# Graph network kernel, first layer: overflow tiles compared out of column numbers in the third section, instead of loaded in the last

## The chip, the core and the metric

One Trainium2 chip, one of its cores. The core has a matrix engine (PE, TensorE), a vector engine (DVE, VectorE), an activation engine (ACT, ScalarE), a general engine (POOL, GpSimd) and a queue engine (SP, SyncE) that here only issues transfers. They run their own instruction streams and meet at semaphores. The metric is device microseconds of one execution, the median of several runs.

## What is computed

Four graph layers over 12,500 nodes with 64 features and 212,500 directed edges, each behind a layer norm and added to x. The second of them (`_L1_gnn_ref`) is the one that matters here: four rounds of a graph convolution over the same graph.

```python
def _L1_gnn_ref(x, edge_index, Ws, bs, ln_w, ln_b):
    deg = jnp.zeros((n,), x.dtype).at[dst].add(1.0) + 1.0
    dinv = jax.lax.rsqrt(deg)
    enorm = (dinv[src] * dinv[dst])[:, None]
    self_norm = (dinv * dinv)[:, None]
    h = x
    for l in range(Ws.shape[0]):
        hw = h @ Ws[l]
        agg = jnp.zeros_like(hw).at[dst].add(enorm * hw[src])
        agg = agg + self_norm * hw + bs[l]
        mean = jnp.mean(agg); var = jnp.mean(jnp.square(agg - mean))
        h = jax.nn.relu(ln_w[l] * (agg - mean) * jax.lax.rsqrt(var + EPS) + ln_b[l])
    return h
```

The last graph layer (`_L2_gnn_ref`) sums messages over the same edges and ends in a small network per node; the kernel does it at the end with the same matrix of edge counts.

## The kernel before, in words

**The matrix.** The kernel sums messages with matrix products. It writes the edges into a dense matrix of counts `adj` in device memory, one byte for each pair of nodes: 98 tiles of 128 source rows by 12,544 columns. A count of 256 or more doesn't fit a byte. Each time a pair's running count reaches a multiple of 256, the kernel writes a one into one of seven more row tiles instead, the overflow tiles (rows 98 to 104 of tiles, `NJ` to `AB`, `NV` = 7). Row p of overflow tile k has at most one such event: `row_f[p, k]` holds the source node, or -1, and `vcol[p, k]` the destination node, which is the column of the one. The stationary operand that goes with overflow tile k is the features of those source nodes times 256; POOL gathers them from `node_table` (`virtual_rows`, line 951) and ACT and DVE split them into three bf16 terms (`virtual_terms`).

**The scatter.** POOL writes the matrix, edges sorted by source row: `adj_out` (line 934) issues 1,664 indirect DMAs of 128 one-byte cells, in NB = 52 blocks of 32. After each block, as it lands, `cells_landed` raises `cells_in`. The order on POOL is: blocks 0 to 14; gathers for another part; blocks 15 to 47; `virtual_rows(0, VT)`; blocks 48 to 51; the last `cells_landed`.

**The first of the four rounds** starts before the scatter is done. Its source rows are cut into nine sections (`CUTS` = 0, 30, 46, 60, 72, 80, 86, 91, 96, 98), and a section's loads on SP wait until the blocks that can touch its rows have landed (`chk`). Each section runs over seven groups of 1,792 destination columns; one section of one group is a unit, and has its own PSUM area of two that alternate. A tile is 128 rows by 1,792 columns, 224 KB of bytes. The path of tile n is: SP loads it to `RAW[n % 5]` (line 770) once the buffer is converted; DVE (n % 5 = 1 or 3) or ACT (0, 2, 4) converts it to bf16 in `RING[n % 5]` once PE has freed that; PE multiplies it in 12 products (`products`, line 1322): three terms, two column parts, two halves. A unit's sum is added to `FM` by `add_part` on DVE; in the last section `scaled` adds it, multiplies by `DINVB` and takes statistics (lines 2596 to 2605). `DINVB` comes by two transfers of SP per group (`group_end`, line 742), which wait until `scaled` has finished the group two before; the loads of the next unit stand behind them in SP's order. PE, too, starts a unit only when the group two before is through `scaled`.

DVE's conversion while POOL scatters is written as a multiply-add with a PSUM operand (line 2558), and as a plain copy (line 2556) from tile `LAST_FROM` = 672 on, which is the first of the last section. The last section has tiles 96 and 97 and the seven overflow tiles, nine per unit, 63 in all. All nine sections together are 735 tiles.

**Behind it** come statistics, three more rounds (lines 1342 and 2669) which load all 105 row tiles per group, and the last graph layer, in which the overflow tiles are already made by a comparison: line 2886 compares column numbers `iota_f` with `srj` (there the source node less 128 times the block number, since that layer sums the other way), a table of 7 by 14 columns that lines 2794 to 2797 make with 98 small instructions just before that layer's tiles.

Of the kernel before, what the change touches and what calls it, by code (L numbers as in the profile page):

```python
# [37 lines left out]
P = 128  # L38
GT = 7
# [28 lines left out]
def gnn_kernel(nc, n_nodes, n_edges, a, out):  # L68
# [22 lines left out]
    NCK = len(CUTS) - 1  # L91
    assert TILES % P == 0 and TILES % CB == 0 and NB % 4 == 0 and CUTS[1] > 0 and CB * P == 1 << 12
# [18 lines left out]
    with ctx:  # L111
# [146 lines left out]
        PART = [list(range(CUTS[c], CUTS[c + 1])) + (list(range(NJ, AB)) if c == NCK - 1 else []) for c in range(NCK)]  # L258
        UNIT = [(c, g) for c in range(NCK) for g in range(NJ // (2 * GT))]
        LAST_OF = [sum(len(PART[c]) for c, _ in UNIT[:u + 1]) - 1 for u in range(len(UNIT))]  # L260
        assert LAST_OF[-1] + 1 == NJ // (2 * GT) * AB
        LAST_FROM = LAST_OF[NJ // (2 * GT) * (NCK - 1) - 1] + 1
        VIRT_AT = LAST_OF[NJ // (2 * GT) * (NCK - 1) - 1] // NR
# [242 lines left out]
        def _(sp):  # L506
# [251 lines left out]
            for c in range(NCK):  # L758
# [4 lines left out]
                for g in range(NG2):  # L763
                    for K in PART[c]:
                        i, r = n % NR, n // NR
                        if i in BY_ACT:
                            sp.wait_ge(sem("conv_a"), r * NA + i // 2 + 1)
                        else:
                            sp.wait_ge(sem("conv_d"), r * ND + i // 2 + 1)
                        sp.dma_start(RAW[i], adj[K * P:(K + 1) * P, g * (2 * QW):(g + 1) * (2 * QW)]).then_inc(sem(f"ring_in{i}"), 16)  # L770
                        n += 1
# [63 lines left out]
        def _(pool):  # L835
# [117 lines left out]
            adj_out(NB // 4 + 2, NB - 4)  # L953
            virtual_rows(0, VT)
            adj_out(NB - 4, NB)
# [29 lines left out]
        def _(pe):  # L985
# [399 lines left out]
            def by_parts():  # L1385

                n = 0
                for u, (c, g) in enumerate(UNIT):
# [6 lines left out]
                    for K in PART[c]:  # L1395
# [8 lines left out]
                        products(stat, RING[i], base, x, K == CUTS[c], K == PART[c][-1]).then_inc(sem("ring_free"), 1)  # L1404
# [586 lines left out]
        def _(dve):  # L1991
# [469 lines left out]
            dve.sem_inc(sem("dve_at"), 1)  # L2461

# [87 lines left out]
            def to_bf16_first(r):  # L2550

                for i in BY_DVE:
                    dve.wait_ge(sem(f"ring_in{i}"), r * 16 + 16)
# [90 lines left out]

            split_terms(0)
            NOTHING = PS[:, 4 * 512:4 * 512 + 1]
            then(dve.memset(NOTHING, 0.0))
            AFTER = {(LAST_OF[u] + NR) // NR: u for u in range(len(UNIT) - 1)}
            assert len(AFTER) == len(UNIT) - 1
            for r in range(NG2 * NK):  # L2650
# [3 lines left out]
                if r in AFTER:  # L2654
                    if UNIT[AFTER[r]][0] < NCK - 1:
                        add_part(AFTER[r])
                    else:
                        scaled(AFTER[r])
# [135 lines left out]
            for k in range(NV):  # L2794
                for j in range(2 * GT):
                    t = dve.tensor_scalar(srj[:, k * 2 * GT + j:k * 2 * GT + j + 1], row_f[:, k:k + 1], float(-j * P), None, ALU.add)
            then(t)
# [153 lines left out]
```

## Time and profile before

| | |
|---|---|
| median of 3 runs | 9879.17 us (9872.16 to 9879.80) |
| the profiled execution, its own time | 9849.77 us |
| its span in the profile | 9847.9 us |
| first round, first product to last | 6040 to 6993 us of the span |
| its last section, first load to last statistics | 6908 to 6997 us |
| PE busy in the span | 7048.5 us (72%) |
| DVE busy | 7017.6 us (71%) |
| ACT busy | 4868.2 us (49%) |
| POOL busy | 5374.9 us (55%) |

The profile's times count from the start of the span. A busy share over the whole span says little here, since the kernel has stages with different limits. One reads first the chain that ended last, then, stage by stage, which engine had no gap and what the others waited for.

### The profile page before, as it was taken

What the parts mean: (1) busy time and instruction counts of PE and PEld (TensorE: products, weight loads), DVE (VectorE), ACT (ScalarE), POOL (GpSimd) and SP (SyncE); (2) the same over time, 40 slices, a digit from 0 to 9 for tenths busy, and PEclk for the clock granted to TensorE, in tenths of its full rate; (3) what the DMA queues carried; (4) which work ended last, traced back from release to release, by engine and by line L of the source; (5) the groups of instructions that cost most, each with busy time, mean ns of one, the idle gap of its engine ahead of it and who ended that gap; (6) DMA issues with size and microseconds to landing.
All of it is one profiled execution on the core that took longest, in us unless ns stands there. A gap on an engine that the chain in (4) does not pass through costs nothing.

```text
span 9847.9 us, 151767 instructions
## 1 busy us (share of the span) xinstructions
PE 7048.5 (72%) x44134; PEld 5763.7 (59%) x44134; DVE 7017.6 (71%) x18590; ACT 4868.2 (49%) x7967; POOL 5374.9 (55%) x5426
## 2 busy tenths in 40 slices
PE   4444444424888878872656567996899999997998
PEld 3333333313666667661445455664699898896887
DVE  7888888833666666662558777775688787787777
ACT  1111111112555555551442336885688787785787
POOL 5777777777777777777777777776000000000220
PEclk5555555555777776775776788998999999998999
DMA  5556544444333333339995896775788888886999
GB/s 192 195 194 196 175 143 143 144 134 66 93 92 93 92 93 93 94 92 93 266 229 123 188 216 175 204 204 123 221 281 281 248 280 252 275 281 177 210 218 198
DMA packets 2775520, 1739.57 MB, mean 177 GB/s; under 512 B 1805046, under 2 KB 2613980, under 8 KB 2774660
## 3 DMA queue, kind: packets, MB, share of 16 engines
q1 hardware_dynamic: 2435460, 1298.36, 52.3%
q10 hardware_dynamic: 165920, 277.72, 8.1%
q0 software_dynamic: 173408, 154.46, 6.8%
q8 instruction: 370, 6.06, 0.3%
q14 instruction: 362, 2.97, 0.1%
HBM read 1065.70 MB, written 506.69 MB: 160 GB/s over the span
## 4 chain that ended last, share of the span: by engine, by line
POOL 44%; PE 19%; issue 18%; DMA 9%; DVE 5%; ACT 3%; SPq 1%; POOLq 0%; DVEq 0%; ACTq 0%
POOL adj L934 16%; POOL records L908 13%; PE PS L1342 13%; POOL G L854 12%; DMA raw_f<-adj 3%; PE PS L1532 3%; DMA pair_raw<-adj 2%; DVE OH L2136 1%; ACT ring_f L1848 1%; DMA G<-node_table,IDX 1%; POOL fill_rows L870 1%; POOL T L885 1%; ACT ring_f L1971 1%; PE PS L1322 1%; POOL AG L885 1%
## 5 line engine op out<-in xcount | busy, mean ns | idle before, releaser
L854 POOL DMA_INDIRECT G<-node_table,IDX x1664 | 1626.1, 977 | 561.8 <-issue 551.3
L934 POOL DMA_INDIRECT adj<-OH,EA x1664 | 1652.5, 993 | 507.3 <-issue 507.3
L908 POOL DMA_INDIRECT records<-RT,IDX x1664 | 1614.0, 970 | 516.8 <-issue 499.6
L1342 PE MATMUL PS<-ring_f,terms_r 128*128 128x448 f32 x8232 | 1702.6, 368 | 17.3 <-DVE ring_f L2669 8.2
L2669 DVE CAST ring_f<-raw_f 128x1792 fp32r<-128x1792 uint8 x1323 | 1408.0, 1091 | 377.7 <-DMA raw_f<-adj 198.6
L1848 ACT CAST ring_f<-raw_f 128x1792 fp32r<-128x1792 uint8 x882 | 1465.5, 1691 | 380.0 <-DMA raw_f<-adj 249.5
L1342 PEld LDWEIGHTS PS<-ring_f,terms_r 128*128 128x128 f32 x8232 | 1537.3, 188 | 172.0 <-ACT ring_f L1848 19.3
L1187 PE MATMUL PS<-R 98*128 98x128 f32 x3328 | 995.1, 392 | 0.0
L2143 DVE TENSOR_TENSOR_SCAN S<-M,S,PS 128x512 f32<-128x512 bf16 x621 | 791.2, 1274 | 249.0 <-ACT PS L1737 224.2
L1102 PE MATMUL PS<-OH 128*98 128x128 bf16 x3328 | 453.3, 316 | 624.0 <-DVE OH L2136 624.0
L951 POOL DMA_INDIRECT HC<-node_table,srow x21 | 31.2, 1486 | 1510.4 <-issue 1510.4
L1102 PEld LDWEIGHTS PS<-OH 128*98 128x98 bf16 x3328 | 365.7, 198 | 781.8 <-DVE OH L2136 781.8
L2136 DVE TENSOR_SCALAR OH<-iota_b,AG 128x128 bf16<-128x128 bf16 (+1 forms) x4480 | 821.5, 283 | 0.0
L1638 ACT ACTIVATE PS<-PS,poolb 128x512 f32<-128x512 f32 x208 | 137.7, 662 | 1311.1 <-PE PS L992 1068.4
L2558 DVE SCALAR_TENSOR_TENSOR AG<-AG,PS 128x1792 bf16<-128x1792 uint8 x269 | 543.1, 2022 | 275.6 <-PE PS L1322 142.5
L2273 DVE TENSOR_TENSOR L<-PS,below 128x512 bf16<-128x512 f32 x416 | 285.7, 687 | 625.4 <-PE PS L1171 619.0
L968 POOL DMA_INDIRECT ends_b<-runs_e,endrow_src x98 | 144.4, 1474 | 1050.6 <-PE PS L1354 548.7
L1187 PEld LDWEIGHTS PS<-R 98*128 98x128 f32 x3328 | 715.3, 265 | 0.0
L1185 PE MATMUL PS<-OH 128*98 128x128 bf16 x1664 | 474.4, 285 | 316.6 <-ACT R L1672 314.9
L992 PE MATMUL PS<-ident,RT 128*128 128x128 f32 x832 | 232.0, 434 | 597.3 <-DVE RT L2160 592.7
L1532 PE MATMUL PS<-ring_f,terms_r 128*128 128x448 f32 x2744 | 608.9, 376 | 66.6 <-DVE ring_f L2883 31.5
L1971 ACT CAST ring_f<-pair_raw 128x1792 fp32r<-128x1792 uint8 x343 | 571.5, 1692 | 167.0 <-PE PS L1532 111.4
(416 smaller groups left out, 14498.8 us busy)
## 6 DMA issues: line engine op xcount, KB each, us to landing
raw_f<-adj SPq DMA_DIRECT2D x2205, 224.0 KB, 3.7
adj<-Z ACTq DMA_DIRECT2D x105, 1568.0 KB
AG<-adj SPq DMA_DIRECT2D x735, 224.0 KB
G<-records SPq DMA_DIRECT2D x624, 128.0 KB
M<-same_dst SPq DMA_DIRECT2D x416, 128.0 KB
fill_rows<-Z ACTq DMA_DIRECT2D x104, 512.0 KB, 2.8
runs_l<-R SPq DMA_DIRECT2D x208, 256.0 KB
G<-fill_rows SPq DMA_DIRECT2D x208, 256.0 KB
```

The source lines that it names most:

```text
L854: pool.indirect_dma_start(G[:, i, q * D:(q + 1) * D], None, table, bass.IndirectOffsetOnAxis(ap=IDX[:, i, q:q + 1], axis=0)).then_inc(sem( ...
L908: pool.indirect_dma_start(rec, bass.IndirectOffsetOnAxis(ap=IDX[:, i, q:q + 1], axis=0), RT[:, i, q, :], None).then_inc(sem(f"scattered{i} ...
L934: pool.indirect_dma_start(adj_cells, bass.IndirectOffsetOnAxis(ap=CELL[:, at:at + 1], axis=0), VAL[:, at:at + 1], None).then_inc(sem(f"cel ...
L1102: t = pe.matmul(hist_of(b, k % 2 if b == 0 else 0), OH[:, s, 2 * b, k, 0:NJ], OH[:, s, 2 * b + 1, k, :], start=False, stop=False, skip_gro ...
L1187: t = pe.matmul(bank(6 + x)[:, k * P:(k + 1) * P], OHTs[0:NJ, x, k * P:(k + 1) * P], Cs[0:NJ, k, :], start=False, stop=True, skip_group_ch ...
L1342: m = pe.matmul(half_of(x, h)[:, c, :], stat, RINGF[q % NR][:, h * QW + c * HW:h * QW + (c + 1) * HW], start=K == 0, stop=False, skip_grou ...
L1532: m = pe.matmul(half_of(0, h)[:, c, :], stat, RINGF[n % NE][:, h * QW + c * HW:h * QW + (c + 1) * HW], start=p == 0, stop=p == AB - 1, ski ...
L1848: act.copy(RINGF[q % NR][:, :], RAWF[q % NW][:, :]).then_inc(sem("conv_a"), 1)
L1971: act.copy(RINGF[n % NE][:, :], raw[:, 0:2 * QW, K % 2]).then_inc(sem("conv_a"), 1)
L2136: t = dve.tensor_scalar(OH[:, s, d, k, 0:w], iota_b[:, 0:w], key(d, q + k), None, ALU.is_equal)
L2143: return dve.tensor_tensor_scan(S[:, i % 2, :], mask, data, init, op0, op1)
L2669: dve.tensor_copy(RINGF[q % NR][:, :], RAWF[q % NW][:, :]).then_inc(sem("conv_d"), 1)
```

## The change

The overflow tiles of the first round are no longer loaded. DVE makes each by one comparison (`scalar_tensor_tensor`: column number `iota_f` plus the group's first column, is-equal `srj`), straight to the ring in bf16. They move from the last section to the third (index `EV_C` = 2), and lie there on ring buffers 1 and 3 alone. A unit of the third section has 21 tiles instead of 14, one of the last 2 instead of 9. SP raises the ring's semaphore for such a tile without a transfer.

So that the operands are there in time: `virtual_rows` moves on POOL from block 48 to block 36 (`EV_AT`), and `virtual_terms` from conversion round 134 to round 64 (`VIRT_AT`). Four small DVE instructions behind `srow_ready` work out `srj` early, from `vcol` (-1 where there is no event). The 98 small instructions before the last graph layer become one. `LAST_FROM` becomes 721. For the last section DVE's finishing of ended units (`close`) is done ahead of the next conversion when the unit's last tile lies five tiles back.

```diff
     NCK = len(CUTS) - 1
+    EV_C = 2
+    EV_AT = NB * 9 // 13
     assert TILES % P == 0 and TILES % CB == 0 and NB % 4 == 0 and CUTS[1] > 0 and CB * P == 1 << 12
...
-        PART = [list(range(CUTS[c], CUTS[c + 1])) + (list(range(NJ, AB)) if c == NCK - 1 else []) for c in range(NCK)]
         UNIT = [(c, g) for c in range(NCK) for g in range(NJ // (2 * GT))]
-        LAST_OF = [sum(len(PART[c]) for c, _ in UNIT[:u + 1]) - 1 for u in range(len(UNIT))]
+
+        def rows_of_units():
+            units, n = [], 0
+            for c, _ in UNIT:
+                nodes, events, rows = list(range(CUTS[c], CUTS[c + 1])), list(range(NJ, AB)) if c == EV_C else [], []
+                while nodes or events:
+                    rows.append((events if rows and events and n % NR in BY_DVE else nodes).pop(0))
+                    n += 1
+                units.append(rows)
+            return units
+
+        PART = rows_of_units()
+        LAST_OF = [sum(len(rows) for rows in PART[:u + 1]) - 1 for u in range(len(UNIT))]
+        EVENT = {sum(len(rows) for rows in PART[:u]) + x: (UNIT[u][1], K - NJ)
+                 for u in range(len(UNIT)) for x, K in enumerate(PART[u]) if K >= NJ}
+        assert len(EVENT) == NV * (NJ // (2 * GT)) and all(n % NR in BY_DVE for n in EVENT)
         assert LAST_OF[-1] + 1 == NJ // (2 * GT) * AB
         LAST_FROM = LAST_OF[NJ // (2 * GT) * (NCK - 1) - 1] + 1
-        VIRT_AT = LAST_OF[NJ // (2 * GT) * (NCK - 1) - 1] // NR
+        VIRT_AT = LAST_OF[NJ // (2 * GT) * EV_C - 1] // NR
...
             spread = [NJ * (k + 1) // NV if g else NJ - NR * (NV - 1 - k) for k in range(NV)]
...
                 for g in range(NG2):
-                    for K in PART[c]:
+                    for K in PART[c * NG2 + g]:
                         i, r = n % NR, n // NR
...
                             sp.wait_ge(sem("conv_d"), r * ND + i // 2 + 1)
-                        sp.dma_start(RAW[i], adj[K * P:(K + 1) * P, g * (2 * QW):(g + 1) * (2 * QW)]).then_inc(sem(f"ring_in{i}"), 16)
+                        if K < NJ:
+                            sp.dma_start(RAW[i], adj[K * P:(K + 1) * P, g * (2 * QW):(g + 1) * (2 * QW)]).then_inc(sem(f"ring_in{i}"), 16)
+                        else:
+                            sp.sem_inc(sem(f"ring_in{i}"), 16)
                         n += 1
...
                         group_end(g, g, g % 2)
...
                                             bass.IndirectOffsetOnAxis(ap=srow[:, k:k + 1], axis=0)).then_inc(sem("vt_in"), 16)
-            adj_out(NB // 4 + 2, NB - 4)
+            adj_out(NB // 4 + 2, EV_AT)
             virtual_rows(0, VT)
-            adj_out(NB - 4, NB)
+            adj_out(EV_AT, NB)
             cells_landed(NB - 1)
...
             with pool.Fori(1, LAYERS) as l:
...
                         pe.wait_ge(sem("part_used"), u - 1)
-                    for K in PART[c]:
+                    for K in PART[u]:
                         i, r = n % NR, n // NR
...
                             pe.wait_ge(sem("conv_a"), r * NA + NA + i // 2 + 1)
...
                         stat = (lambda t: TERMS[t][:, K * D:(K + 1) * D]) if K < NJ else (lambda t: VT3[:, t, (K - NJ) * D:(K - NJ + 1) * D])
-                        products(stat, RING[i], base, x, K == CUTS[c], K == PART[c][-1]).then_inc(sem("ring_free"), 1)
+                        products(stat, RING[i], base, x, K == CUTS[c], K == PART[u][-1]).then_inc(sem("ring_free"), 1)
                         n += 1
...
                             own(g, x)
...
             dve.sem_inc(sem("dve_at"), 1)
+            then(dve.tensor_scalar(vrow[:, :], row_f[:, :], 0.0, None, ALU.is_ge))
+            then(dve.scalar_tensor_tensor(vcol[:, :], vcol[:, :], 1.0, vrow[:, :], ALU.add, ALU.mult))
+            then(dve.tensor_scalar(vcol[:, :], vcol[:, :], -1.0, None, ALU.add))
+            then(dve.scalar_tensor_tensor(srj.rearrange("p (k j) -> p k j", j=2 * GT), rowbc(iota_f[:, 0:2 * GT], NV), float(-P),
+                                          bc(vcol[:, :], [P, NV, 2 * GT]), ALU.mult, ALU.add))
...
                 for i in BY_DVE:
+                    while ended[0] < len(UNIT) and LAST_OF[ended[0]] + NR <= r * NR + i:
+                        close(ended[0])
+                        ended[0] += 1
+                    if r * NR + i in EVENT:
+                        g, k = EVENT[r * NR + i]
+                        dve.wait_ge(sem("ring_free"), r * NR + (i + 1))
+                        dve.scalar_tensor_tensor(RING[i].rearrange("p (j c) -> p j c", c=P), rowbc(iota_f[:, :], 2 * GT), float(g * 2 * QW),
+                                                 bc(srj[:, k * 2 * GT:(k + 1) * 2 * GT], [P, 2 * GT, P]),
+                                                 ALU.add, ALU.is_equal).then_inc(sem("conv_d"), 1)
+                        continue
                     dve.wait_ge(sem(f"ring_in{i}"), r * 16 + 16)
...
                     if r * NR + i >= LAST_FROM:
...
+            def close(u):
+                if UNIT[u][0] < NCK - 1:
+                    add_part(u)
+                else:
+                    scaled(u)
+
             split_terms(0)
...
             then(dve.memset(NOTHING, 0.0))
-            AFTER = {(LAST_OF[u] + NR) // NR: u for u in range(len(UNIT) - 1)}
-            assert len(AFTER) == len(UNIT) - 1
+            AFTER = {(LAST_OF[u] + NR) // NR: u for u in range(len(UNIT) - NG2 - 1)}
+            assert len(AFTER) == len(UNIT) - NG2 - 1
+            ended = [len(UNIT) - NG2 - 1]
             for r in range(NG2 * NK):
...
                 if r in AFTER:
-                    if UNIT[AFTER[r]][0] < NCK - 1:
-                        add_part(AFTER[r])
-                    else:
-                        scaled(AFTER[r])
+                    add_part(AFTER[r])
+            while ended[0] < len(UNIT) - 1:
+                close(ended[0])
+                ended[0] += 1
             statistics(0, scaled(len(UNIT) - 1))
...
                 dve.sem_inc(sem("joined"), 1)
...
             dve.tensor_tensor(fold, ident[:, 0:D], ident[:, D:P], ALU.add)
-            for k in range(NV):
-                for j in range(2 * GT):
-                    t = dve.tensor_scalar(srj[:, k * 2 * GT + j:k * 2 * GT + j + 1], row_f[:, k:k + 1], float(-j * P), None, ALU.add)
-            then(t)
+            then(dve.scalar_tensor_tensor(srj.rearrange("p (k j) -> p k j", j=2 * GT), rowbc(iota_f[:, 0:2 * GT], NV), float(-P),
+                                          bc(row_f[:, :], [P, NV, 2 * GT]), ALU.mult, ALU.add))
             dve.wait_ge(sem("pair_used"), UD + NG2)
...
             dve.wait_ge(sem("carry"), 48)
```

## Rows read from the trace of the kernel before

**Rows 1.** The page: the chain that ended last (part 4).

```profile
POOL 44%; PE 19%; issue 18%; DMA 9%; DVE 5%; ACT 3%; SPq 1%; POOLq 0%; DVEq 0%; ACTq 0%
POOL adj L934 16%; POOL records L908 13%; PE PS L1342 13%; POOL G L854 12%; DMA raw_f<-adj 3%; PE PS L1532 3%; DMA pair_raw<-adj 2%; DVE OH L2136 1%; ACT ring_f L1848 1%; DMA G<-node_table,IDX 1%; POOL fill_rows L870 1%; POOL T L885 1%; ACT ring_f L1971 1%; PE PS L1322 1%; POOL AG L885 1%
```

**Rows 2.** Busy us by engine in stretches; PEclk is the granted clock.

```profile
6043.00:6729.00 686.00, 683.35 (x7213) 455.81 (x7208) 523.68 (x280) 592.58 (x360) 521.66 (x540) 1.00 0.71 201
6729.00:6758.00 29.00, 0.24 (x4) 0.00 (x0) 0.00 (x0) 0.15 (x1) 21.99 (x24) 0.60 0.09 20
6758.00:6806.00 48.00, 44.54 (x642) 28.91 (x644) 34.52 (x21) 34.48 (x21) 36.55 (x38) 0.92 0.55 158
6806.00:6840.00 34.00, 5.41 (x80) 3.25 (x74) 0.95 (x2) 0.79 (x1) 25.94 (x27) 0.65 0.09 20
6840.00:6908.00 68.00, 38.99 (x360) 20.83 (x360) 31.05 (x19) 30.39 (x19) 24.39 (x26) 0.75 0.80 106
6908.00:6998.00 90.00, 81.20 (x816) 47.86 (x816) 58.02 (x63) 66.23 (x43) 0.00 (x0) 0.96 0.71 218
```

**Rows 3.** Chain in order of time, 6690 to 7060: start, us, what.

```profile
6836.80 2.92 DMA AG<-adj
...
6872.27 34.67 DMA AG<-adj
```

**Rows 4.** Timeline of POOL: start, us, line, instruction [idle before].

```profile
5408.40 0.97 POOL L934 DMA_INDIRECT adj<-OH,EA  x1 [0.30 <-issue]
5409.67 6.70 POOL L934 DMA_INDIRECT adj<-OH,EA  x1 [0.30 <-issue]
5416.67 6.42 POOL L934 DMA_INDIRECT adj<-OH,EA  x1 [0.30 <-issue]
```

**Rows 5.** Timeline of DVE in the same stretch.

```profile
5408.84 6.69 DVE L2073 TENSOR_TENSOR Hn<-X,nd 128x6272 f32<-128x6272 f32 x1
5415.56 6.69 DVE L2074 TENSOR_TENSOR AG<-Hn 128x6272 f32<-128x6272 f32 x1
```

**Rows 6.** Timeline of POOL beside two broadcast operands.

```profile
5988.00 1.70 POOL L934 DMA_INDIRECT adj<-OH,EA  x1 [0.30 <-issue]
```

**Rows 7.** Timeline of DVE there.

```profile
5987.77 1.08 DVE L2524 TENSOR_TENSOR R<-vneg,crow 128x896 f32<-128x896 f32 x1
```

**Rows 8.** Timeline of DVE in the second section: start, us, idle before.

```profile
6198.54 2.02 DVE L2558 SCALAR_TENSOR_TENSOR AG<-AG,PS 128x1792 bf16<-128x1792 uint8 x1 [1.38 <-PE PS L1322]
6200.81 2.02 DVE L2558 SCALAR_TENSOR_TENSOR AG<-AG,PS 128x1792 bf16<-128x1792 uint8 x1 [0.25 <-PE PS L1322]
```

**Rows 9.** Single lines: ns min, median, max; first to last start.

```profile
L2886 DVE TENSOR_TENSOR ring_f<-iota_f,below x49: 2006/2020/2028, 9141.8 to 9831.3; 128x1792 fp32r<-128x1792 f32 x49
...
L2796 DVE TENSOR_SCALAR below<-row_f x98: 144/146/149, 9062.0 to 9067.9; 128x1 f32<-128x1 f32 x98
...
L951 POOL DMA_INDIRECT AG<-node_table,srow x7: 941/944/987, 6700.5 to 6708.0; - x7
```

**Rows 10.** Timeline of SP: the first load of the last section.

```profile
6908.43 0.33 SPq L770 DMA_DIRECT2D AG<-adj  x1
```

**Rows 11.** Timeline of DVE, the unit of group 3 and the last statistics.

```profile
6950.52 1.08 DVE L2596 TENSOR_TENSOR Hn<-PS,Hn 128x896 f32<-128x896 f32 x1
6951.64 1.09 DVE L2597 TENSOR_TENSOR Hn<-Hn,Z 128x896 f32<-128x896 f32 x1
...
6996.60 0.51 DVE L2603 BATCH_NORM_STATS2 BN<-Hn 64x6 f32<-64x340 f32 x1
```

**Rows 12.** Timeline of SP behind that unit: start, us.

```profile
6952.59 1.09 SPq L742 DMA_DIRECT2D Z<-dinv_n  x2
```

**Rows 13.** Chain: the load behind it.

```profile
6953.72 5.34 DMA AG<-adj
```

**Rows 14.** Chain, 9035 to 9150.

```profile
9062.07 5.36 DVE below L2796 x88
...
9068.03 1.10 DVE ring_f L2883
```

## The prediction

> **What bounds the kernel now.** I read the chain first. POOL has 44% of it, and its scatter of the matrix, line 934, is the longest single entry with 16% [rows 1]. So what holds POOL up while it scatters is paid in full. Next the busy times by stretch, from the first product of the first round on [rows 2]. From 6043 to 6729 us PE has no gap (683.4 of 686.0 us, clock at full): 7,213 products are 602 tiles of 12, or 1.14 us a tile; these are sections 1 to 6. Then PE idles some 29 us, does the seventh section (6758 to 6806), idles some 34 us, and does the eighth. Over the two gaps POOL goes on scattering and the load share is 0.09: PE waits for the matrix. The chain says the same: the eighth section's first load goes out at 6836.80, behind a scatter [rows 3]. The last scatter is issued at about 6872; a load issued at 6872.27 takes 34.67 us [rows 3], and PE works only 39 of the 68 us from 6840 to 6908 [rows 2]. The first load of the last section goes out at 6908.43 [rows 10] and its last statistics end at 6997.1 [rows 11]: a tail of 88.7 us after the matrix is complete, for 63 tiles, with PE busy 81 of 90 us [rows 2].
>
> So two things set the end of this round: when the scatter ends, and how long the last section takes behind it.
>
> **1. Work moved into the third section.** 49 tiles of 1.14 us are 56 us more for PE, in a part where it has no gap. PE would be through the sixth section at 6729 + 56 = 6785, where now it waits until 6758. The seventh needs 45 us (44.5 busy, [rows 2]), to 6830, before the gate of the eighth at 6836.8. The gap of 34 us takes up what is left: this costs nothing even if the scatter isn't delayed, with 7 us in hand. DVE keeps its two tiles in each round of five: a tile now takes 2.02 us [rows 8], and the comparison of the same 128x1792 elements in the last layer takes 2.02 too [rows 9]. The 49 loads on SP go (0.33 us of queue and 224 KB each) where nobody waited for them: nothing. `virtual_rows` ran at 6700 [rows 9]; 12 blocks of 32 scatters of 1.27 us earlier (686.0/540, [rows 2]) is 6212. PE needs the terms at tile 322, 6043 + 322 x 1.14 = 6410, so there are about 200 us in hand, and the tables they read are written before the first section starts. The seven gathers cost POOL the same in the new place. DVE's four small instructions behind `srow_ready` cost it 1 us at most, far from any path; POOL is released before them.
>
> **2. What the comparison does to POOL.** The conversion it replaces reads one operand in SBUF and one in PSUM, and over 686 us of it a scatter lasts 521.66/540 = 0.97 us [rows 2]. The comparison reads two in SBUF. The trace has such instructions beside the scatter. DVE's line 2073, two SBUF inputs, runs 5408.84 to 5415.53 [rows 5]; the scatter started at 5409.67 lasts 6.70 us, to 5416.37 [rows 4]. The next falls into line 2074 (to 5422.25) and ends at 5423.09. Both end 0.84 us after DVE does. With operands broadcast as in the change it is the same: line 2524 ends at 5988.85 [rows 7], and the scatter around it at 5989.70 [rows 6]. So a scatter reads its list 0.13 us (0.97 - 0.84) after it starts, and if it finds a two-input instruction running there it waits for its end. The Trainium skill says this in "SBUF — State Buffer", "Who interferes with whom": a Vector instruction with two SBUF inputs contends with a GpSimd instruction that reads SBUF. By that rule, too, the trace agrees.
>
> The price: scatters come every 1.27 us, a comparison lasts 2.02, so each catches exactly one. At least 2.02 - 0.15 - 1.27 = 0.6 us is lost (0.15 us is my allowance for its start, by estimate), at most 1.87. The phase isn't free, because a held scatter is released with DVE's end, and the next ones read 1.27 and 2.54 us after that. DVE's two tiles of a round start 0.25 and 1.38 us after the one before [rows 8]. The first comparison of a pair catches the reading at 1.27 and ends at 2.27: 1.00 us lost. The second starts at 1.38, just behind that reading, catches the one at 2.54 and ends at 3.40: 0.86. Mean 0.93. I take some 40 of the 49 at that, and 9 that follow a node tile or an `add_part` at the middle of the bounds, 1.23: 37 + 11 = 48 us. Ends: 49 x 0.6 = 29 and 49 x 1.87 = 92. The scatter is on the chain, so the last gates and the end of the matrix shift by this: **+48 us**. PE's extra 56 us hide below it.
>
> **3. The last section.** After the change it has 14 tiles. PE would need 16 us, so something else bounds it. DVE has per unit `scaled`, from 6950.52 to 6952.73 [rows 11], and 1.15 us of statistics: 3.4 us, and 0.9 for its share of conversions; 30 us for seven. But the order on SP bounds it further. The loads of unit g+1 stand behind `group_end(g)`, which waits for `scaled` of g-2. Before, the step from the end of `scaled` (6952.73) over SP's two transfers (6952.59 to 6953.7, [rows 12]) to the landing of the next load (6959.06, [rows 13]) took 6.3 us; with conversion 1.1 and `scaled` 2.2 a round trip is 9.7 us. It can be laid out from DVE's order: conversion of tile 726, `scaled` 0; 728, `scaled` 1 and 2; 731, `scaled` 3; 733, `scaled` 4, 5, 6. Tile 726 can only be loaded once 721 is converted: two loads of 3 to 5 us, two conversions and one `scaled` set `scaled` 0 at about 15.5 us. Then round trips for 1, 3 and 4 (29 us), and three times 3.4 us for 2, 5 and 6, and the longer last statistics, 1.7: 15.5 + 29 + 10 + 1.7 = 56 us, against 88.7: **-32 us**. Ends: DVE alone, about 40 us, is -48; a round trip for every unit, 15.5 + 6 x 9.7 + 1.7 = 75, is -13.
>
> **4. The small table before the last layer.** 98 instructions from 9062.07 to 9068.03 stand on the chain, and the conversion behind them holds PE [rows 14, 9]. One of 98 elements, some 0.2 us, replaces them: 5.8 us, of which part meets transfers that are late next: **-5** (ends -6 and -2).
>
> **5. The clock.** In the last section PE now has 16 us of work in 56, and the granted clock fell to 0.60 and 0.65 in the idle gaps [rows 2]. The slower products hide in the section, but the second round starts on that clock: I allow **+1** (0 to 4).
>
> **Sum.** 48 - 32 - 5 + 1 = +12 us on the profiled execution's 9849.8 gives 9862. That execution is 29 us (0.3%) below the median of the timed runs, so the same difference on 9879.2 gives **9891 us**.
>
> **The rivals.**
> - *POOL isn't held by this form.* Then the scatter ends as before, PE is just in time, and it is -32 - 5 + 1 = -36: 9843. Against it: line 2524 has broadcast inputs and held a scatter [rows 6, 7]. For it: the output is bf16 and the instruction has an added constant, which no row shows beside a scatter in the same way. 0.12.
> - *The hold is for whole instructions on both sides (slower).* Then a comparison could only start between two scatters, always just behind the end of one, and the next would wait for all but 0.30 us of it: 49 x 1.72 = 84 us, or 84 - 36 = +48: 9927. It decides from 1.15 us a comparison on, where the sum passes +20. Against it: line 2073 starts at 5408.84 inside the scatter of 5408.40 and lasts the same 6.69 us as line 2074 [rows 4, 5]. 0.12. The same section of "SBUF — State Buffer" in the Trainium skill has this rule, that whoever issues first has the shared ports for its whole instruction and the other is blocked; these rows speak against it.
> - *The last section pays a round trip for every unit.* The tail is 75 us, the sum 48 - 13 - 5 + 1 = +31: 9910. Transfers may land later than they did behind one another. 0.12.
> - *The last section is bound by DVE alone.* The sum is 48 - 48 - 5 + 1 = -4: 9875. It needs loads that are always there; SP's order speaks against it. 0.09.
>
> **How the numbers follow.** My forecast, +12, has 0.55, with its own range of 9867 to 9915 (POOL 29 to 66 us, tail -25 to -38). The first rival is faster; so is a twentieth of the forecast. The second and third, and a fifth of the forecast, lie over +20. About 0.2%, 20 us, is what a measurement of this kernel can tell from no change. So faster 0.15, same 0.50, slower 0.35. The range takes in both the first rival and the second in part: 9848 to 9926.
>
> **What would show it.** In the profile after: comparisons of about 2.02 us, 49 of them between 6410 and 6580; beside each a scatter of 1.8 to 2.0 us instead of 0.97, and line 934's total up by some 48 us; the last scatter at about 6920 instead of 6872; the gap before the seventh section shorter, about 20 us, and that before the eighth as now; again some 35 us between last scatter and the first load of the last section; from that load to the last statistics about 56 us with waits for loads on DVE; line 2796's 6 us gone. If scatters stay at 0.97 us the first rival holds. If comparisons themselves are stretched, the second. Wrong altogether would be a wait of PE for `virt_ready`, or a gap in PE before 6729 + 56.

## The result, and the profile after

| | before | after |
|---|---|---|
| median of the timed runs | 9879.31 us (16 runs, 9870.8 to 9896.3) | 9902.27 us (16 runs, 9883.51 to 9914.03) |
| after / before | | 1.0019 (95%: 1.0012 to 1.0025), +23 us |
| profiled execution | 9849.77 us | 9907.16 us |
| POOL's time in the 1,664 scatters | 1652.5 us | 1701.0 us |
| last scatter of the matrix starts | 6871.0 us | 6917.7 us |
| first load of the last section | 6908.43 us | 6972.21 us |
| last statistics of the round end | 6997.1 us | 7027.06 us |
| from that load to those statistics | 88.7 us | 54.9 us |

The kernel became slower by 23 us, 0.19%; I had forecast 12. The two profiled executions differ by more than the timed medians, by 57 us: 30 up to the last statistics, and 27 behind them. The profiled execution of before was shorter than any timed one, and how far the part behind varies from one execution to the next is taken up with the sum below.

What the comparisons cost POOL is in three places. First DVE's line itself (duration in ns min, median, max; first and last start):

```profile
L2583 DVE SCALAR_TENSOR_TENSOR AG<-iota_f,below x49: 2018/2026/2099, 6439.1 to 6600.0; 128x1792 bf16<-128x1792 f32 x49
  PE PS L1341: 30.7, 45
```

All 49 stand in the third section, have a median of 2.03 us, and what they wait for is a free ring buffer: their own duration isn't stretched, but for two of 2.10 us that the last section of this document comes back to. POOL's timeline of the same stretch is (start, us, line, idle before):

```profile
6449.96 1.96 POOL L953 DMA_INDIRECT adj<-OH,EA  x1 [0.30 <-issue]
6452.23 0.97 POOL L953 DMA_INDIRECT adj<-OH,EA  x1 [0.30 <-issue]
6453.50 1.83 POOL L953 DMA_INDIRECT adj<-OH,EA  x1 [0.30 <-issue]
6455.63 1.97 POOL L953 DMA_INDIRECT adj<-OH,EA  x1 [0.30 <-issue]
6457.91 0.96 POOL L953 DMA_INDIRECT adj<-OH,EA  x1 [0.30 <-issue]
```

and DVE's:

```profile
6452.47 2.03 DVE L2583 SCALAR_TENSOR_TENSOR AG<-iota_f,below 128x1792 bf16<-128x1792 f32 x1 [1.38 <-PE PS L1341]
6454.73 2.03 DVE L2583 SCALAR_TENSOR_TENSOR AG<-iota_f,below 128x1792 bf16<-128x1792 f32 x1 [0.24 <-PE PS L1341]
6458.54 2.02 DVE L2592 SCALAR_TENSOR_TENSOR AG<-AG,PS 128x1792 bf16<-128x1792 uint8 x1 [1.78 <-DMA AG<-adj]
```

The scatter of 6452.23 had begun 0.24 us before the comparison and stays at 0.97. The next, begun inside the comparison, lasts until 6455.33, 0.83 us past DVE's end at 6454.50; the one after it until 6457.60, 0.84 past 6456.76. Beside the conversion of 6458.54, whose second operand is in PSUM, scatters are short again. Over the whole trace, the 49 comparisons hold 49 scatters, one each, and each of these ends 0.84 or 0.85 us behind its comparison. The profile page's group of the whole line:

```profile
L953 POOL DMA_INDIRECT adj<-OH,EA x1664 | 1701.0, 1022 | 507.3 <-issue 506.1
```

The second piece is the end of the round. The chain in order of time:

```profile
6883.97 4.55 DMA AG<-adj
...
6918.08 44.44 DMA AG<-adj
...
6976.58 4.11 DMA AG<-adj
...
6991.37 3.42 DMA AG<-adj
...
7002.66 3.90 DMA AG<-adj
...
7010.97 3.67 DMA AG<-adj
...
7018.40 4.30 DMA Z<-dinv_n
```

The gate of the eighth section, its first load at 6883.97, lies 47.2 us later than before [rows 3], as the scatter does. The load that goes out beside the last scatters takes 44.44 us where it was 34.67 [rows 3]; I call it the held load. The last section's tiles, 63 before, are 14, and between them stand four landings and the scales: SP's order bounds the section. Its first load:

```profile
6972.21 0.33 SPq L787 DMA_DIRECT2D AG<-adj  x1
```

PE in stretches (columns as in [rows 2]):

```profile
6600.00:6770.00 170.00, 170.00 (x1800) 101.88 (x1798) 136.12 (x75) 148.12 (x91) 129.47 (x133) 1.00 0.73 204
6840.00:6880.00 40.00, 27.25 (x402) 17.35 (x396) 15.13 (x9) 15.22 (x10) 30.48 (x32) 0.91 0.27 72
6880.00:6918.00 38.00, 23.62 (x216) 12.96 (x218) 22.14 (x13) 20.73 (x13) 28.85 (x31) 0.78 0.63 148
6918.00:6966.00 48.00, 10.95 (x88) 4.99 (x82) 6.53 (x5) 7.16 (x5) 0.71 (x1) 0.60 0.82 28
6966.00:7030.00 64.00, 39.09 (x291) 19.41 (x292) 40.03 (x50) 20.18 (x13) 0.00 (x0) 0.77 0.51 143
```

There is no gap left before the seventh section, where there were 29 us; its extra tiles fill that together with a start of the first round that was late by chance (c_after keeps a gap of 13 us there). PE still waits before the eighth, 21.6 us from 6870.0 on, so the scatter, not PE, sets this part. From 6918 to 6966 little runs, with the DMA engines 0.82 busy at 28 GB/s: that is the wait of 44 us for the held load.

### The profile page after: what moved, and what is told of

The parts are those of the page before. It is cut to its first block, busy times and chain, and to the rows that moved or that the text cites. A ratio compares the mean times of both kernels' runs of the same rounds, so it can differ in the third digit from the quotient of the medians.

```text
span 9905.4 us, 151625 instructions
## 1 busy us (share of the span) xinstructions
PE 7087.2 (72%) x44134; PEld 5745.3 (58%) x44134; DVE 7032.0 (71%) x18497; ACT 4876.9 (49%) x7967; POOL 5427.3 (55%) x5426
## 4 chain that ended last, share of the span: by engine, by line
POOL 43%; PE 18%; issue 18%; DMA 11%; DVE 6%; ACT 3%; SPq 1%; POOLq 0%; ACTq 0%; DVEq 0%
POOL adj L953 17%; POOL records L927 12%; PE PS L1361 12%; POOL G L873 11%; DMA raw_f<-adj 3%; DMA pair_raw<-adj 3%; PE PS L1551 2%; DVE OH L2155 2%; DMA G<-node_table,IDX 1%; ACT ring_f L1867 1%; POOL fill_rows L889 1%; ACT ring_f L1990 1%; POOL AG L904 1%; DMA records<-RT,IDX 1%; DMA IDX<-in_src_q 1%
## 5 line engine op out<-in xcount | busy, mean ns | idle before, releaser
L953 POOL DMA_INDIRECT adj<-OH,EA x1664 | 1701.0, 1022 | 507.3 <-issue 506.1
L2592 DVE SCALAR_TENSOR_TENSOR AG<-AG,PS 128x1792 bf16<-128x1792 uint8 x239 | 482.1, 2021 | 241.9 <-PE PS L1341 127.9
```

The costliest lines, as they stand in the source:

```text
L953: pool.indirect_dma_start(adj_cells, bass.IndirectOffsetOnAxis(ap=CELL[:, at:at + 1], axis=0), VAL[:, at:at + 1], None).then_inc(sem(f"cel ...
```

## The experiments

Each group ran on one chip beside the kernel before, whose median was 9903.91 us on the first (10 runs), 9889.48 on the second (25) and 9868.82 on the third (15). Where stages are compared I take them from the start of the first scatter, since what lies ahead of it starts by chance some 20 us earlier or later. So the kernel before has three more profiles, here c_before, c_before_2 and table_alone (its first round is the same).

### Whether the two profiles repeat

Both kernels unchanged, one profiled execution each on the first chip, and the kernel before once more on the third.

> The kernel before once more, for a second profile: which of the differences between the two profiles outside the first round are only from one execution to the next. If the start of the first round (6040 us before, 6066 after) and the last graph layer (762 us from its first conversion to its last before, 786 after) vary by themselves, this profile shows other values for them than the first one; the scatter's end at 6872 us and the 88.7 us behind the first load of the last section should repeat within some 3 us.

> The changed kernel once more, for a second profile. What comes from the change repeats: last scatter at about 6918 us, then some 53 us to the first load of the last section, then 55 us to its last statistics. If the late start of the first round (6066 us) comes from the change it repeats too; if it is chance it does not.

> The kernel before once more, for a third profile, on the same chip: how far the last layer's 762 and 775 us and the first round's start (6040 and 6052 us) go from one execution to the next. If they are chance, a value up to 786 and 6066 is to be expected; if the kernel before really has a shorter last layer, it stays below 776.

The three executions took 9869.48 us (c_before), 9929.16 (c_after) and 9871.80 (c_before_2). From first scatter to last scatter: 2291.7 us in the profile of before, then 2290.9, 2290.0 and (table_alone) 2289.4; with the change 2338.5, and 2345.5 in c_after. From last scatter to last aggregation of statistics: 126.3, 131.2, 125.6, 127.9 before; 109.5 and 99.9 after. So the scatter's delay repeats within 7 us, and what follows it moves by 10. The first round began at 6053 and 6064 us in the two new profiles of before, and 6070 in c_after, so its start is chance. Two things came out otherwise than expected. In c_after the last section's first load goes out 44.4 us behind the last scatter, not 53; the table under "Units that end at ring place 0" takes that apart. And the last layer took 775.5 and 770.4 us in the two new profiles of before, so that it stayed below 776 there, which I had put down as the sign of a shorter last layer in the kernel before; but pads_spread and hold_alone, with the same last layer, have 784 and 786. The profile page's group of the scatter in c_before and c_after:

```profile
L934 POOL DMA_INDIRECT adj<-OH,EA x1664 | 1652.7, 993 | 507.3 <-issue 507.3
```

```profile
L953 POOL DMA_INDIRECT adj<-OH,EA x1664 | 1706.6, 1026 | 507.7 <-issue 507.7
```

### The comparison with one operand in PSUM

Theory A: the second SBUF operand holds POOL. Theory B: something else in the move does.

```diff
             then(dve.memset(NOTHING, 0.0))
+            SRP = PS[:, 5 * 512:5 * 512 + NV * 2 * GT]
+            then(dve.tensor_copy(SRP, srj))
...
-                                                 bc(srj[:, k * 2 * GT:(k + 1) * 2 * GT], [P, 2 * GT, P]),
+                                                 bc(SRP[:, k * 2 * GT:(k + 1) * 2 * GT], [P, 2 * GT, P]),
```

> The changed kernel, but the table of columns is copied to PSUM once (98 columns) and the comparison reads it there, so that it has one operand in SBUF instead of two. Theory A (a comparison with two SBUF operands holds POOL's scatter): scatters beside it last 0.97 us again, the last one starts at about 6871 instead of 6918, and the time falls by some 45 us against the changed kernel, to about 9857 us, 22 below the kernel before. Theory B (the scatter is late for another reason, the earlier row gathers or the DMA queues): nothing changes, about 9902 us.

Measured 9874.35 us (6 runs), 0.997 of before (0.9957 to 0.9982), -30 us: the only difference to the change is where 98 columns lie, and its +23 is gone. DVE's line and the profile page's group:

```profile
L2583 DVE SCALAR_TENSOR_TENSOR AG<-iota_f,PS x49: 2015/2020/2021, 6409.4 to 6570.3; 128x1792 bf16<-128x1792 f32 x49
```

```profile
L953 POOL DMA_INDIRECT adj<-OH,EA x1664 | 1651.3, 992 | 507.2 <-issue 507.2
```

POOL's timeline beside the comparison of 6451.12, of 2.02 us:

```profile
6450.74 0.96 POOL L953 DMA_INDIRECT adj<-OH,EA  x1 [0.31 <-issue]
6452.01 0.97 POOL L953 DMA_INDIRECT adj<-OH,EA  x1 [0.30 <-issue]
6453.28 0.96 POOL L953 DMA_INDIRECT adj<-OH,EA  x1 [0.30 <-issue]
```

No scatter is held, the comparison is as long as before, and first to last scatter is 2289.9 us again. This is also the state that the first rival described (-36): with the scatter as fast as before, -30 was measured. PE's 56 us are hidden even so, but only just. It has no gap of over 3 us from the first product of the round to 6866 us, so that of the 7 us in hand nothing is left, and it is nonetheless no later than in the change once the held load has landed (the table under "Units that end at ring place 0").

### The hold alone

The kernel before, in which 49 of DVE's conversions add their zero out of SBUF instead of PSUM.

```diff
-                        dve.scalar_tensor_tensor(RING[i], RAW[i], 1.0, NOTHING.broadcast_to([P, 2 * QW]), ALU.mult, ALU.add).then_inc(sem("conv_d"), 1)
+                        none = NONE_SB if r * NR + i in HELD else NOTHING
+                        dve.scalar_tensor_tensor(RING[i], RAW[i], 1.0, none.broadcast_to([P, 2 * QW]), ALU.mult, ALU.add).then_inc(sem("conv_d"), 1)
...
+            NONE_SB = below[:, 0:1]
+            then(dve.memset(NONE_SB, 0.0))
+            HELD = [n for n in range(LAST_OF[2 * NG2 - 1] + 1, AB * NG2) if n % NR in BY_DVE][:49]
```

> The kernel before, nothing moved; in the third section and behind it, the conversions of 49 successive DVE tiles add a zero from SBUF instead of one from PSUM. They read two SBUF operands for 2.02 us each, and nothing else differs. Theory A: each lengthens one scatter by 0.86 or 1.0 us, the last scatter starts some 46 us later, and the whole kernel is slower by about the same, some 9925 us. Theory B: no difference, 9879 us.

Measured 9948.6 us (5 runs), 1.0044 of before (1.003 to 1.0057), +45 us, with 1702.2 us in the scatters. A stretch of POOL and DVE there:

```profile
6449.83 0.97 POOL L934 DMA_INDIRECT adj<-OH,EA  x1 [0.30 <-issue]
6451.10 1.82 POOL L934 DMA_INDIRECT adj<-OH,EA  x1 [0.31 <-issue]
6453.23 1.96 POOL L934 DMA_INDIRECT adj<-OH,EA  x1 [0.30 <-issue]
```

```profile
6450.06 2.02 DVE L2559 SCALAR_TENSOR_TENSOR AG<-AG,below 128x1792 bf16<-128x1792 uint8 x1 [1.38 <-PE PS L1322]
6452.33 2.03 DVE L2559 SCALAR_TENSOR_TENSOR AG<-AG,below 128x1792 bf16<-128x1792 uint8 x1 [0.24 <-PE PS L1322]
```

The same pattern without any comparison: the operand's place does it, in an 8-bit multiply-add as in a comparison. And 50 us on POOL are 45 us in the kernel's time.

### What holds the load behind the last scatter

The last scatters write the padding: 492 edges beyond the 212,500. Each of them, like each edge whose pair comes again right behind it, writes to a byte of its own in a row that nobody reads, and these bytes are neighbours. Theory C: many one-byte writes to neighbouring bytes hold the transfers behind them. Theory D: it is the scatter's end itself, whatever its addresses.

```diff
-                then(dve.tensor_tensor(own, own, own_col, ALU.subtract))
+                then(dve.scalar_tensor_tensor(own, own, 7.0, own_col, ALU.mult, ALU.subtract))
```

The kernel before, with the bytes 7 apart.

> The kernel before; only the cells into which repeats of one pair are written, a row that nobody reads, lie 7 bytes apart instead of side by side. The last 492 edges are padding, all of one pair, so that the last four scatters write 128 neighbouring bytes each. Theory C (these writes to the same few bytes' surroundings hold up memory for the 35 to 45 us behind the last scatter, in which loads take up to 34 us): the hold-up falls to a fraction, 5 to 15 us, and the time by 20 to 35 us against the kernel before. Theory D (it is how long any scatter's writes take to drain, or the loads collide with all of them): the hold-up stays at 35 to 45 us and the time within 5 us.

Measured 9864.32 us (9 runs), 0.9976 of before (0.9966 to 0.9986), -25 us; last scatter to last aggregation 98.9 instead of 126 to 131. Traffic behind the last scatter, first with the change (6920 to 6960), then here (6870 to 6910):

```profile
DMA packets 663, 0.98 MB, mean 25 GB/s; under 512 B 122, under 2 KB 662, under 8 KB 662
...
q1 hardware_dynamic: 601, 0.97, 87.3%
```

```profile
DMA packets 4675, 7.79 MB, mean 195 GB/s; under 512 B 609, under 2 KB 4416, under 8 KB 4672
...
q1 hardware_dynamic: 4604, 7.74, 76.4%
```

With neighbouring bytes the DMA queue is 87% busy and moves 25 GB/s; the kernel before moves 31 GB/s there (c_before, 6866 to 6906). With the bytes apart it moves 195 GB/s in the same place. Only addresses were changed, so C stands. What in the memory takes the time isn't shown. The edit also spreads the bytes of other repeated pairs; that the padding's 492 do it is argued from where the hold lies. The chain behind the last scatter now has only a load of 6.87 us:

```profile
6872.68 6.87 DMA AG<-adj
6879.57 2.02 DVE AG L2558
```

### Units that end at ring place 0

With 49 tiles more ahead of them, the units of sections 7 and 8, five tiles each, end at another place of the ring of five buffers. DVE's rows of the change in the eighth section:

```profile
6902.46 2.02 DVE L2592 SCALAR_TENSOR_TENSOR AG<-AG,PS 128x1792 bf16<-128x1792 uint8 x1 [1.49 <-PE PS L1341]
6904.73 2.02 DVE L2592 SCALAR_TENSOR_TENSOR AG<-AG,PS 128x1792 bf16<-128x1792 uint8 x1 [0.25 <-PE PS L1341]
6906.67 1.08 DVE L2677 TENSOR_TENSOR Hn<-PS,Hn 128x896 f32<-128x896 f32 x1
6909.24 2.02 DVE L2592 SCALAR_TENSOR_TENSOR AG<-AG,PS 128x1792 bf16<-128x1792 uint8 x1 [1.49 <-PE PS L1341]
```

`add_part` comes only behind both conversions, PE waits for it, and a unit takes 6.78 us (6909.24 - 6902.46). The waits of 6750 to 6870 list `PE PS L1341 <- DVE Hn L2677` with 6.3 us in 7 times. The experiment closes every unit ahead of the next conversion, as the change does in its last section only:

```diff
-            AFTER = {(LAST_OF[u] + NR) // NR: u for u in range(len(UNIT) - NG2 - 1)}
-            assert len(AFTER) == len(UNIT) - NG2 - 1
-            ended = [len(UNIT) - NG2 - 1]
+            AFTER = {}
+            ended = [0]
```

> The changed kernel, with DVE finishing every ended unit ahead of the next conversion that lies five tiles behind it, instead of at the end of the round except in the last section. Theory E (the 49 tiles put into the third section shift where units end in the ring of five, so that in sections 7 and 8 PE waits for add_part once a unit: 6.8 us for 5 tiles instead of 5.7): a unit there takes 5.7 us again, fewer tiles are left when the scatter ends, and the time falls by 5 to 10 us against the changed kernel, 9892 to 9897 on the chip of the first measurement, +13 to +18 against the kernel before. If the alignment doesn't matter: +23 as before.

Measured 9909.28 us (11 runs), 1.0020 of before (1.001 to 1.0029), +20. In its profile a unit takes 5.68 us:

```profile
6902.18 2.02 DVE L2592 SCALAR_TENSOR_TENSOR AG<-AG,PS 128x1792 bf16<-128x1792 uint8 x1 [0.25 <-PE PS L1341]
6904.38 1.09 DVE L2677 TENSOR_TENSOR Hn<-PS,Hn 128x896 f32<-128x896 f32 x1 [0.18 <-PE PS L1341]
...
6907.86 2.02 DVE L2592 SCALAR_TENSOR_TENSOR AG<-AG,PS 128x1792 bf16<-128x1792 uint8 x1 [0.25 <-PE PS L1341]
```

and last scatter to aggregation is 95.9 us. The three profiles that have the change's tail as it is show 109.5, 99.9 and (psum_operand) 110.0. What moves these is the held load, and the traces let one take it out. Here it lands at 6958.32, and the last section's first load follows at once:

```profile
6918.98 39.34 DMA AG<-adj
...
6960.44 0.33 SPq L787 DMA_DIRECT2D AG<-adj  x1
```

The same three steps in all profiles, in us:

| profile | last scatter's start to the held load's landing | from there to the last section's first load | from the landing to the last aggregation |
|---|---|---|---|
| before | 35.9 | 1.5 | 90.3 |
| c_before | 39.2 | 2.5 | 92.0 |
| c_before_2 | 35.8 | 0.3 | 89.8 |
| table_alone | 38.3 | 1.9 | 89.6 |
| hold_alone | 43.2 | 0.3 | 91.3 |
| the change | 44.8 | 9.7 | 64.7 |
| c_after | 35.7 | 9.7 | 64.2 |
| psum_operand | 46.2 | 9.7 | 63.8 |
| loads_first (below) | 35.0 | 7.8 | 48.7 |
| close_ahead | 38.9 | 2.1 | 57.1 |

The first step varies in both kernels. The second is 8 to 10 us wherever units end at place 0 and are closed late, and at most 2.5 elsewhere. So closing them late costs the round 7 to 8 us, and close_ahead takes that away. In the timed runs it can't be seen: +20, with an interval of +10 to +29, can't be told from +23, and the +13 to +18 that I expected lie inside it too.

### Loads ahead of the scales

```diff
-                    if c == NCK - 1:
-                        group_end(g, g, g % 2)
+                    if c == NCK - 1 and g:
+                        group_end(g - 1, g - 1, (g - 1) % 2)
+            group_end(NG2 - 1, NG2 - 1, (NG2 - 1) % 2)
```

The change, in which SP issues a unit's loads before it waits for the group two back.

> The changed kernel, but in the last section SP issues the loads of unit g+1 ahead of the two transfers of group g. Theory F (the last section is bound by the round trip over SP, as forecast): the 55 us from its first load to its last statistics fall to 40 or 45, since a unit's loads no longer wait for the statistics of two groups before, and the kernel is 10 to 15 us faster than the changed one, +8 to +13 against the kernel before. If DVE or the transfers of the scales bound it: no difference from the changed kernel, +23.

Measured 9895.88 us (11 runs), 1.0007 of before (0.9998 to 1.0016), +6. The section's first load goes out at 6966.46 and its last statistics end at 7007.25: 40.8 us, against 54.9. The time is 17 us better than the change's by the two differences to the kernel before, where I expected 10 to 15. The section's middle on DVE's timeline:

```profile
6982.55 1.08 DVE L2591 CAST AG<-AG 128x1792 bf16<-128x1792 uint8 x1
6983.54 1.08 DVE L2631 TENSOR_TENSOR Hn<-PS,Hn 128x896 f32<-128x896 f32 x1
6984.66 1.09 DVE L2632 TENSOR_TENSOR Hn<-Hn,Z 128x896 f32<-128x896 f32 x1
6985.78 1.15 DVE L2640 BATCH_NORM_STATS2 BN<-Hn 128x6 f32<-128x512 f32 x2
6986.85 1.07 DVE L2631 TENSOR_TENSOR Hn<-PS,Hn 128x896 f32<-128x896 f32 x1
```

DVE has no gap here. So in the change it is SP's order that bounds the section. With that gone DVE does, at about the 40 us which the fourth rival took for it.

### The small table alone

The kernel before with the one instruction in place of the 98.

```diff
-            for k in range(NV):
-                for j in range(2 * GT):
-                    t = dve.tensor_scalar(srj[:, k * 2 * GT + j:k * 2 * GT + j + 1], row_f[:, k:k + 1], float(-j * P), None, ALU.add)
-            then(t)
+            then(dve.scalar_tensor_tensor(srj.rearrange("p (k j) -> p k j", j=2 * GT), rowbc(iota_f[:, 0:2 * GT], NV), float(-P),
+                                          bc(row_f[:, :], [P, NV, 2 * GT]), ALU.mult, ALU.add))
```

> The kernel before; only the table of columns ahead of the last graph layer is made by one instruction instead of 98. Theory G (the 98 stand on the path, as forecast): from the last statistics of the fourth round to the first conversion of the last layer 95 us instead of 100, and the last layer itself as before (the profiles so far: 762 to 786 us), so 5 us faster, which the timing can hardly tell from nothing. Theory H (what is gained there is given back in the last layer, whose loads set its pace): 95 us, but a last layer of some 5 us more, and no gain in time.

Measured 9869.93 us (11 runs), 1.0001 of before (0.9992 to 1.001): no difference, within 10 us. The instruction takes 0.25 us:

```profile
L2794 DVE SCALAR_TENSOR_TENSOR below<-iota_f,row_f x1: 254/254/254, 9066.6 to 9066.6; 128x98 f32<-128x98 f32 x1
```

From the last aggregation of statistics to the last layer's first conversion on DVE it is 93.5 us; the five profiles with the old table have 99.8 to 100.2, the six others with the new one 94.0 to 95.4. So 5 to 6 us are won up to there. But the last layer's own stretch, first to last such conversion, was 762 to 786 us with the old table (five profiles, mean 776) and 779 to 790 with the new (seven, mean 786). Its spread is larger than the gain, and the means lean to theory H, which gives the gain back there. Whether the gain reaches the end stays open.

### All four together

The change with the operand in PSUM, the bytes 7 apart, every unit closed ahead, and the loads ahead of the scales.

> All four together in the changed kernel: the table in PSUM, units finished ahead, loads of the last section first, repeats 7 bytes apart. If they add up: -30 (the table in PSUM, measured against the kernel before) -8 -12 -25 = some 75 us faster than the kernel before; less where the scatter's end no longer comes last, since PE is then through the seventh section only just before the gate of the eighth (at least -50).

Measured 9809.05 us (5 runs, 9806.37 to 9811.04), 0.9920 of before (0.9906 to 0.9933), -80 us. The last scatter starts at 6873.4 and the last aggregation at 6925.8, 52.4 us behind it, where the kernel before has 126 to 131. The chain there:

```profile
6877.13 6.83 DMA AG<-adj
...
6889.60 6.16 DMA AG<-adj
...
6917.19 4.42 DMA Z<-dinv_n
```

It beats both kernels, and -75 had been expected. Against the change it is 103 us less, by the two differences to the kernel before; the profiles of the first round, from first scatter to last aggregation, have 2341.9 us here and 2448.0 there, 106 less.

## Why the prediction was right

**The hold on POOL (forecast +48).** Right in mechanism and size. The pattern on POOL is the one laid out from [rows 4 to 8]: in a pair of comparisons one scatter of 1.83 and one of 1.97 us, so 0.86 and 1.00 lost, each ending 0.84 us behind DVE. 38 of the 49 held scatters have these two durations, where I took 40; the others lost 1.0 us on average, not 1.23, and 0.66 to 1.57 singly. The line's total rose by 48.5 us in this profile, and by 50 to 54 in c_after and the experiments that keep it. psum_operand takes it away alone and hold_alone brings it alone. The rule of the Trainium skill ("SBUF — State Buffer", "Who interferes with whom") that a Vector instruction with two SBUF inputs contends with a reading GpSimd instruction agrees with both: the scatters take 1651.3 us with one of the inputs in PSUM and 1701.0 us with both in SBUF.

**The hold for whole instructions on both sides (rival at 0.12).** It falls: 47 of the 49 comparisons start inside a scatter and take 2.03 us at most, and the pair's gaps are still 0.24 and 1.38 us. The measurement decides against the rule that the prediction set beside this rival. That POOL isn't held by this form falls as well.

**PE's 56 us (forecast 0).** Right, by less than I thought. It has no gap from 6600 to 6770 us and waits for the eighth section all the same. The first round began 27 us later than in the profile of before (first product 6067 against 6041); over all profiles it begins anywhere from 6035 to 6070, so this is chance, and there was room for it too. Without the delay of the scatter (psum_operand) no gap was left: the forecast of 7 us in hand was too high. `virtual_rows` ran from 6212.0 us on, as laid out, and nothing waited for it.

**The last section (forecast -32, tail 56 us).** From its first load to the last statistics 54.9 us, so the layout of round trips held, and loads_first shows that it was SP's order: 40.8 us without it, the end that was taken for DVE alone.

**What failed: "again some 35 us between last scatter and the first load of the last section".** That was 36.4 us before (6908.43 - 6872.0, the last scatter's end) and 53.5 after (6972.21 - 6918.7). I had carried the number over without asking what it consists of. It has two parts (table above). One is the hold behind the padding's bytes, which pads_spread explains: it lasts until 35 to 46 us behind the last scatter, whichever kernel, and the mean of the two profiles of the change is 3 us above that of the four of before, which is within its spread. The other is what comes between the held load and the last section's first load: 9.7 us instead of 1.5, since PE, with 6.78 instead of 5.68 us a unit, had some five more tiles of the eighth section to do when the scatter ended (17 of 35, against 12), and each unit was closed late. close_ahead shows this part back at 2.1 us. Where units end in the ring after 49 tiles have moved was in no term of the sum, and it cost 8 us.

**The sum.** In these two profiles the statistics come 46.7 + 17.1 - 33.8 = +30 us later, against my 48 - 32 = +16. Over the two profiles of the change and the four of before, the scatter gives +51.5, the stretch up to the last section's first load +11, and the last section -34: +28. (With psum_operand among the profiles behind the scatter it is +30.) With -5 for the table, if it lasts, that is +23 to +25, and +23 was measured. The forecast of +12 was 11 short, by the stretch just named for the most part, and by 3.5 us of scatter.

That the sum meets +23 so closely is partly luck. It takes what lies behind the round's last aggregation as unchanged but for the table, and executions differ there by more than the whole effect: 2850.7, 2871.9 and 2870.5 us in the three profiles of the kernel before, 2886.8 and 2889.2 in hold_alone and pads_spread, which have the same instructions there, and 2878.1 and 2884.0 in the two of the change. Whether the change costs or saves anything there is open.

**The table (-5)** came up to the last layer as forecast; that it reaches the end isn't shown. **The clock (+1)**: it was 0.77 in the last section (0.96 before, [rows 2]), and the three rounds behind took 1979.0 us. The same rounds took 1970.6 us in the profile of before, and 1978.9 to 1988.5 in the five other profiles with that kernel's last section, so an effect of 1 us can't be seen.

## What to carry to other kernels

When work moves to VectorE beside GpSimd's indirect DMAs, look at where its operands lie before you count its time. Here a second SBUF input cost the scatter 1 us each time, the same input in PSUM cost it nothing, and one instruction moved the 98 columns there. Of a stretch that a forecast carries over "as before", ask what it is made of. And when many padding elements must be written somewhere, spread their addresses.

## What the runs showed of the hardware

- An indirect DMA of 128 one-byte cells takes 0.97 us of GpSimd. Beside VectorE instructions with two SBUF inputs it is held if it began more than about 0.04 us after such an instruction did, while that was running, and then ends 0.84 us behind it: in each of the five profiles that have such instructions in the first round, 49 of them hold 49 scatters. Begun earlier, 0.24 us before the instruction for instance, it is free. VectorE isn't held in turn by a scatter that is under way. Only when a scatter began 0.04 us after the VectorE instruction and stayed free was that one longer, 2.10 instead of 2.02 us: three times among the 245 of the five profiles. I had taken the hold from instructions in float32; it holds for an 8-bit input and for a bf16 output as well.
- Behind 492 one-byte writes to neighbouring addresses a load of 224 KB lands only 35 to 46 us after the last scatter's start, with a DMA queue 87% busy at 25 GB/s. With 7 bytes from one to the next the loads go at 195 GB/s, and the kernel gains 25 us. That 7 is enough was seen; other distances were not run.
